# Opening of a fused two-layer transformer kernel: VectorE's work of the first token rounds reordered, setup work moved between rounds and engines, filler transposes on TensorE

## The reference, cut to what matters

```
x = x + xattn0(ctx, layernorm(x), mask, ...)   # heads 8 x 64; queries from x, keys and values from ctx and x; l2norm of q and k
x = x + int8_ffn(layernorm(x), weight_q, ...)  # per-row quantised 128x128 product
x = x + xattn1(layernorm(x), ctx, We, W2)      # softmax over the query axis
x = x + moe_ffn(layernorm(x), Wr, W1, W2, ...) # argmax over 8 experts, 128 -> 512 -> 128 with relu
```

```
def layer_norm(x, w, b): ... (x - mu) * rsqrt(var + LN_EPS) * w + b
def l2norm(t): t / max(sqrt(sum(t*t)), L2_EPS)
q = latents @ Wq ; k, v = split(concat([x, latents]) @ Wkv)
q = l2norm(q) * q_scale ; k = l2norm(k) * k_scale
out = softmax(where(mask, q k^T * SCALE, -max)) v ; layer_norm(out @ Wo)
```

## Time and profile before

| | |
|---|---|
| median of 3 runs | 961.88 us |
| the profiled execution | 963.69 us |
| its span in the trace | 962.0 us |
| TensorE busy | 913.5 us, 95% of the span |
| VectorE, ScalarE, GpSimd busy | 748.6, 691.3, 464.9 us |
| chain of waits, share on TensorE | 69% |

### The profile page before, as it was taken

How to read it: one execution, slowest core, us unless ns; L and a number is a source line. 1 busy time by engine, 2 the same in 40 slices (tenths; PEclk the granted TensorE clock), 3 DMA queues, 4 the chain that set the end, 5 groups by cost and what they waited for, 6 DMA issues and landing times.

```text
span 962.0 us, 30865 instructions
## 1 busy us (share of the span) xinstructions
PE 913.5 (95%) x11222; PEld 802.9 (83%) x11222; DVE 748.6 (78%) x2524; ACT 691.3 (72%) x1655; POOL 464.9 (48%) x1093
## 2 busy tenths in 40 slices
PE   3899999999999999999999999999999999899997
PEld 2688888888888888888888888888888878899997
DVE  4666788888888888888888888888888878868553
ACT  2777778777777777777777777777778766676764
POOL 4333333454545454544454444445453544767554
PEclk9999999999999999999999999999999999999999
DMA  6742000000000000000000000000000012246310
GB/s 180 219 132 38 2 3 1 3 13 3 13 2 13 3 10 5 14 2 8 7 11 5 8 7 8 7 8 8 8 8 7 8 47 70 60 90 111 96 52 21
DMA packets 45195, 31.45 MB, mean 33 GB/s; under 512 B 11556, under 2 KB 40167, under 8 KB 45047
## 3 DMA queue, kind: packets, MB, share of 16 engines
q1 hardware_dynamic: 39446, 19.93, 8.9%
q0 software_dynamic: 4320, 8.50, 2.8%
q10 hardware_dynamic: 1280, 1.05, 0.4%
HBM read 17.75 MB, written 12.17 MB: 31 GB/s over the span
## 4 chain that ended last, share of the span: by engine, by line
PE 69%; DVE 15%; ACT 9%; issue 3%; POOL 2%; SPq 1%; DMA 0%; DVEq 0%; POOLq 0%; ACTq 0%
PE ps L1622 9%; PE ps L1579 7%; PE ps L1554 7%; PE ps L1668 7%; PE ps L1533 5%; PE ps L1541 5%; PE ps L1376 5%; PE ps L1378 5%; PE ps L1377 5%; DVE sumsq L1271 4%; PE ps L1627 3%; ACT qk_hat L595 2%; PE ps L1652 2%; ACT probs L588 2%; PE ps L1415 1%
## 5 line engine op out<-in xcount | busy, mean ns | idle before, releaser
L1579 PE MATMUL ps<-v_x,prob 128*64 128x65 f32 x2048 | 130.6, 227 | 6.3 <-ACT qq_t L646 2.8
L655 ACT ACTIVATE prob<-ps,neg_shift 128x512 f32<-128x512 f32 x128 | 88.4, 691 | 67.0 <-PE ps L1622 66.8
L1271 DVE TENSOR_REDUCE sumsq<-qk_hat 128x8 f32<-128x512 f32 x168 | 108.4, 678 | 32.9 <-ACT qk_hat L595 30.6
L1303 DVE TENSOR_TENSOR qk_hat<-ps,rstd 128x512 f32<-128x512 f32 x168 | 106.3, 684 | 33.5 <-POOL rstd L826 32.6
L819 POOL TENSOR_TENSOR rs_t<-rs_y 128x32 f32<-128x32 f32 x73 | 17.7, 242 | 226.3 <-ACT rs_y L634 226.3
L1579 PEld LDWEIGHTS ps<-v_x,prob 128*64 128x64 f32 x2048 | 104.9, 137 | 25.2 <-issue 14.1
L1579 PE MATMUL ps<-v_c,prob 128*64 128x65 f32 x2048 | 125.7, 222 | 0.0
L1376 PE MATMUL ps<-w_hi,xc_hi 128*128 128x512 f32 x272 | 119.0, 438 | 2.4 <-POOL xc_lo L793 2.4
L595 ACT ACTIVATE qk_hat<-ps 128x512 f32<-128x512 f32 x168 | 98.7, 599 | 29.9 <-PE ps L1378 22.5
L1622 PE MATMUL ps<-qT_all,kT_all 64*128 64x128 f32 x1536 | 111.6, 285 | 2.9 <-ACT w_all L604 1.2
L1378 PE MATMUL ps<-w_hi,xc_lo 128*128 128x512 f32 x272 | 107.6, 395 | 0.0
(11 more groups left out here) (237 smaller groups left out, 2260.5 us busy)
## 6 DMA issues: line engine op xcount, KB each, us to landing
x_res<-sorted_rows SPq DMA_DIRECT2D x71, 65.5 KB
w_all<-in_L_ffn_W_dram SPq DMA_DIRECT2D x16, 256.0 KB, 4.8
sorted_rows<-fill SPq DMA_DIRECT2D x8, 327.5 KB
out_dram<-prob,x_res POOLq DMA_INDIRECT x71, 2.3
sorted_rows<-stage,idx POOLq DMA_INDIRECT x64, 2.4
ctx_res<-in_ctx_dram SPq DMA_DIRECT2D x8, 115.5 KB
x_res<-in_x_dram SPq DMA_DIRECT2D x1, 768.0 KB
sorted_rows<-fill SPq DMA_DIRECT2D x1, 524.0 KB, 5.1
```

What stands on the lines that cost most here:

```text
L655: nc.scalar.activation(prob[:, n // 2, n % 2 * INNER:(n % 2 + 1) * INNER], ps_s[n], ACT.Exp, bias=(mask_now[:, par:par + 1] if n > 1 else ...
L1271: nc.vector.reduce_sum(sumsq[:, n * H:(n + 1) * H], sq[:, n * INNER:(n + 1) * INNER].rearrange("p (h d) -> p h d", d=DH), AX).then_inc(ss_ ...
L1303: nc.vector.tensor_tensor(qk_hat[:, n * INNER:(n + 1) * INNER].rearrange("p (h d) -> p h d", d=DH), ps_qk[:, n, :].rearrange("p (h d) -> p ...
L1579: last = nc.tensor.matmul(dst[half:half + DH, :], prob[:, kt, col + half:col + half + DH], v, start=kt == 0, stop=kt == 1)
```

## The change

VectorE: `split_weights` is cut in two. The cast to `w_hi` waits until GpSimd has written the first variance (`var_ready` 1); `w_lo` is made after block 0's `xc_hat`, in three instructions of 512 columns. Statistics of block 2 and the sums of squares of block 0 move from round -1 to the end of round -2's middle part, ahead of the wait for `rs_ready` 2 and ahead of `xc_hat` of block 1. The copies of the turned expert weights are shared out anew: VectorE takes numbers 2 and 3, ScalarE 0, 1, 4 and 5, number 0 before the logarithm of round -1, 1 behind it, 4 and 5 at the end of the round.

TensorE: turns of experts 0 and 1 come before the transposes of `xc_hat` of block 1. The three transposes of the second layers, with ScalarE's copies of them, move from round 0 to round `SECOND_J` = 5. The wait for `setup_v` 12 moves to the second v product of round 0; ScalarE waits for `setup_v` 10 only. `keep_busy(48)` and `keep_busy(14)` issue transposes of the identity into PSUM bank 0 before round -2 and before round -1.

GpSimd: the memset of lot 2's context moves between the variance and the Newton step of round -1, the constants of the second layers behind that Newton step. SP: `arrived(1)` moves up from behind expert 2 to behind expert 1.

```diff
@@ SP
             for e in range(AHEAD):
                 expert(e)
-            arrived(1)
+                if e == 1:
+                    arrived(1)
@@ ScalarE
-            def first_weights():
+            def first_weights(some):
                 for n, bank, w in first_flips():
-                    if n > 1:
+                    if n in some:
                         act.wait_ge(s["wT_done"], n + 1)
                         nc.scalar.activation(w, ps[:, bank, :], ACT.Copy).then_inc(s["w_copied"], 1)
...
                 if not inside and j == 0:
-                    act.wait_ge(setup_v, SETUP_V)
+                    act.wait_ge(setup_v, SHIFT_V)          # 10
...
+                if not inside and j == -1:
+                    first_weights((0,))
                 roots()
...
                 if not inside and j == -1:
-                    first_weights()
+                    first_weights((1,))
...
+                if not inside and j == -1:
+                    first_weights((4, 5))
@@ GpSimd
                     last.then_inc(var_ready, 1)
+                    if not inside and j == -1:
+                        nc.gpsimd.memset(ctx_res[:, packed[2], :], 0.0).then_inc(ctx_zeroed, 1)
...
                     nc.gpsimd.tensor_tensor(rstd[:, par, :], rs_t4[:, :], rs_t3[:, :], ALU.mult).then_inc(rs_ready, 1)
+                if not inside and j == -1:
+                    second_setup()                         # L860 to L869 of before
                 if inside or j != -2:
                     high_low()
...
             run(-2, 0, 0, -2, False, -2, 0)
-            nc.gpsimd.memset(ctx_res[:, packed[2], :], 0.0).then_inc(ctx_zeroed, 1)
-            ...
@@ VectorE
-            def split_weights():
+            def high_weights():
                 dve.wait_ge(ld_qkv, 32)
+                dve.wait_ge(var_ready, 1)
                 nc.vector.tensor_copy(w_hi[:, :], w_raw[:, :]).then_inc(setup_v, 1)
+            def low_weights():
                 dve.wait_ge(setup_v, 2)
-                nc.vector.tensor_tensor(w_lo[:, :], w_raw[:, :], w_hi[:, :].bitcast(F32), ALU.subtract).then_inc(setup_v, 1)
+                for n in range(3):
+                    part = slice(n * INNER, (n + 1) * INNER)
+                    last = nc.vector.tensor_tensor(w_lo[:, part], w_raw[:, part], w_hi[:, part].bitcast(F32), ALU.subtract)
+                last.then_inc(setup_v, 1)
...
+            def sums_of_squares(j, pos):
+                for n in range(3) if fresh(pos + 1) else range(2):
+                    dve.wait_ge(sq_done, 3 * j + 4 + n)
+                    nc.vector.reduce_sum(...).then_inc(ss_raw, 1 if n == 0 or fresh(pos + 1) else 2)
+                dve.wait_ge(ss_raw, 3 * j + 6)
+                if j == -1:
+                    dve.wait_ge(rs_ready, 2)
+                nc.vector.tensor_scalar(var_in[:, 0:3 * H], sumsq[:, :], L2_EPS * L2_EPS, None, ALU.max).then_inc(ss_done, 1)
+            def third_tokens():
+                dve.wait_ge(tokens_in, 3)
+                nc.vector.bn_stats(bn6[:, 0, :], one(x_res, 2)).then_inc(xc_bn, 1)
+                dve.wait_ge(xc_bn, 3)
+                nc.vector.bn_aggr(xc_stat[:, 0, 0, :], bn6[:, 0, :]).then_inc(xc_mv, 1)
...
                 if not inside and j == -3:
-                    split_weights()
+                    high_weights()
                 if not inside and j == -2:
                     scales()
+                    third_tokens()
+                    sums_of_squares(-1, -1)
...
                     last.then_inc(hat_ready, 1)
+                if not inside and j == -3:
+                    low_weights()
@@ TensorE
-                if not inside and j == 0:
+                if not inside and j == SECOND_J:
                     pe.wait_ge(s["setup_d"], 1)
-                    pe.wait_ge(s["w_copied"], 4)
-                    pe.wait_ge(setup_v, SETUP_V)
                     nc.tensor.transpose(g_three[:, 0, :], wq_f, ident[:, :])
...
                     for kt in (0, 1) if fresh(pos) else (0,):
+                        if not inside and j == 0 and kt == 1:
+                            pe.wait_ge(setup_v, SETUP_V)
...
+                if not inside and j == -1:
+                    first_weights((0, 1, 2, 3))
                 if has(j + 2, inside):
                     pe.wait_ge(hat_ready, j + 3)
...
+            def keep_busy(n):
+                for i in range(n):
+                    nc.tensor.transpose(ps[:, 0, 0:P], ident[:, :], ident[:, :])
+
             pe.wait_ge(setup_g, FIRST_G)
             run(-3, 1, 3, -3, False, -3, 0)
+            keep_busy(48)
             run(-2, 0, 0, -2, False, -2, 0)
+            keep_busy(14)
...
-                    for n, bank, w in first_flips():
-                        pe.wait_ge(ld_exp[n // 2], 32)
-                        if n > 3:
-                            pe.wait_ge(s["w_taken"], n - 3)
-                        flip(bank, w).then_inc(s["wT_done"], 1)
-                    pe.wait_ge(s["w_copied"], 1)
+                    first_weights((4, 5))                  # waits w_copied 1, 2
+                    pe.wait_ge(s["w_taken"], 1)
                     pe.wait_ge(setup_v, 4)
```

More of the change, by code:

```diff
@@ L304, in whole @@
         SETUP_V, SETUP_G, FIRST_G = 12, 9, 7
+        SHIFT_V = 10
+        SECOND_J = E - AHEAD
         SETUP_P = 10
@@ L730, in _, with second_setup @@
             pool.wait_ge(setup_g, FIRST_G)
+            def second_setup():
+                nc.gpsimd.memset(upper_f, 1.0).then_inc(setup_p, 1)
+                nc.gpsimd.iota(rev_i[:, :], pattern=[[-1, E]], base=E, channel_multiplier=0).then_inc(setup_p, 1)
+                nc.gpsimd.iota(part_i[:, :], pattern=[[PART, E]], base=0, channel_multiplier=0).then_inc(setup_p, 1)
+                nc.gpsimd.iota(table["iota_i"][:, :], pattern=[[1, table["iota_i"].shape[1]]], base=0,
+                               channel_multiplier=0).then_inc(setup_p, 1)
+                nc.gpsimd.iota(table["base_i"][:, :], pattern=[[PART, E]], base=0, channel_multiplier=0).then_inc(setup_p, 1)
+                nc.gpsimd.memset(before[:, :], 0.0).then_inc(setup_p, 1)
+                nc.gpsimd.memset(ones_pp[:, :], 1.0).then_inc(setup_p, 1)
+                pool.wait_ge(setup_p, 7)
+                nc.gpsimd.affine_select(out=upper_f, in_=upper_f, compare_op=ALU.is_gt, fill=0.0,
+                                        base=0, pattern=[[1, P]], channel_multiplier=-1).then_inc(setup_p, 1)
             def store(k):
@@ L1220, in run @@
                     dve.wait_ge(o_bn, j - 1)
-                if has(j + 3, inside):
+                if has(j + 3, inside) and (inside or j != -1):
                     dve.wait_ge(tokens_in, j + 4)
@@ L1237, in run @@
                                                    lno_w[:, :], ALU.subtract, ALU.mult).then_inc(o_cent, 1)
-                elif has(j + 3, inside):
+                elif has(j + 3, inside) and (inside or j != -1):
                     dve.wait_ge(xc_bn, j + 4)
-                if has(j + 3, inside):
+                if has(j + 3, inside) and (inside or j != -1):
                     for n in (0, 1) if fresh(pos + 3) else (0,):
@@ L1267, in run @@
                     first_table(j, 0)
[L1268 to L1272, removed]
-                                             AX).then_inc(ss_raw, 1 if n == 0 or fresh(pos + 1) else 2)
-                    dve.wait_ge(ss_raw, 3 * j + 6)
-                    nc.vector.tensor_scalar(var_in[:, 0:3 * H], sumsq[:, :], L2_EPS * L2_EPS, None,
-                                            ALU.max).then_inc(ss_done, 1)
+                if has(j + 1, inside) and (inside or j != -1):
+                    sums_of_squares(j, pos)
                 if not tail(j, inside):
@@ L1390, in flip, with first_weights @@
                 return last
+            def first_weights(some):
+                for n, bank, w in first_flips():
+                    if n in some:
+                        pe.wait_ge(ld_exp[n // 2], 32)
+                        if n > 3:
+                            pe.wait_ge(s["w_copied"], n - 3)
+                        flip(bank, w).then_inc(s["wT_done"], 1)
             def slot_a(j, rho, g, inside):
-                if not inside and j == 0:
+                if not inside and j == SECOND_J:
                     pe.wait_ge(s["setup_d"], 1)
-                    pe.wait_ge(s["w_copied"], 4)
-                    pe.wait_ge(setup_v, SETUP_V)
                     nc.tensor.transpose(g_three[:, 0, :], wq_f, ident[:, :])
@@ L1503, in three_emptied @@
                     pe.wait_ge(s["w_copied"], 4 + 2 * j + 2)
+                if not inside and j == SECOND_J:
+                    pe.wait_ge(s["setup_c"], 3)
                 for at, name, of in ((0, "place_done", g - 2), (1, "pr_done", g - 1), (2, "qt_copied", g),
```

9 lines of the change are left out of this document (7 added, 2 removed).

## The result

The changed kernel takes 959.0 us (median of 6 runs, 957.82 to 959.71) against 963.13 us of the kernel before (6 runs beside it on the same chip): ratio 0.9961, 95% interval 0.995 to 0.9971, so 2.8 to 4.8 us faster. The forecast of 956.9 us was counted from a median of three runs, 961.88; beside the changed kernel, with six runs, the kernel before has 963.13, so 1.25 us of the distance between 956.9 and 959.0 lie in the starting point and 0.9 in the gain. On two other chips the gain was 4.0 us (977.97 against 981.92, ratio 0.9957, 0.9941 to 0.9973) and 3.5 us (980.25 against 983.71, ratio 0.9956, 0.9942 to 0.9969). The profiled execution takes 959.33 us, its span is 957.6 us, 4.4 less than before.

What follows compares the result with a forecast made beforehand. Opening bound by a chain of latencies up to the first v product at 28.28 us, TensorE afterwards; 5.9 - 0.5 - 0.4 = 5.0 us gained, 961.88 - 5.0 = 956.9 us; range 955.4 to 961.0, the forecast's own 956.0 to 958.5.

Steps and rivals of the forecast that it cites:

- part 5: Round 0 on TensorE: a stall of 0 to 1.1 us for expert 3's second load, taken as -0.4 us.
- Part 1: Weight split leaves GpSimd's first variance undisturbed: first Newton step 2.0 us earlier, block 0's products 2.1 us earlier.
- Part 2: Fillers raise TensorE's clock early: block 0's nine passes take 2.1 instead of 3.7 us, `var_in` 4.1 us earlier.
- rival 1: The filler transposes never raise TensorE's clock: gain only 1.0 us, 960.9 us; chance 0.15.
- rival 2: TensorE's clock rises, then falls in the gaps before block 0's products: gain 3.8, 958.1 us; chance 0.11.
- Rivals 3 and 4: Fillers each wait for the last's drain, 963.0 us, chance 0.06; GpSimd's disturbance only moved, 958.0 us, 0.09.
- Parts 3 and 4: VectorE fills the Newton wait, `qk_hat` 4.1 us earlier; setup leaves round 0, v product 5.9 us earlier, round 5 loses 0.5.
- The slip of SP: Moving `arrived(1)` ahead of expert 2 delays everything behind it on SP by 0 to 1.0 us, taken as 0.5.
- the landing: Expert 3's second load takes 4.8 us from issue to landing, so it lands at 23.3 to 23.8 us.

Runs made afterwards that it cites:

- the undisturbed trace: The changed kernel itself run again on another chip, its clock not dropping in the opening: 977.97 us, against 981.92 for the kernel before.

## Why the prediction was right, and where it was off

It said 5.0 us; the medians give 4.1, 4.0 and 3.5, and a pair of traces without clock stretches in the opening 3.6. The mechanism was right: the v product came early, by the links named, and a short wait for expert 3 took part of it back. The term that was mis-sized most is that wait, part 5. By its steps:

- Part 1, 2.0 us at the Newton step: 1.6. The variance was written at 7.8 as worked out, and GpSimd was not slowed by VectorE (0.1 us of the gain is that lot 0 came earlier in this trace). The term was mis-sized because I took ScalarE as free at 7.9, and its queue held mask loads until 8.40. Before, the late variance had hidden them.
- Part 2: the products came at 14.2 (forecast 13.9), at the high level, `var_in` at 17.91 (17.73). The clock rose under transposes alone, so rival 1 fell; the Trainium skill (TensorE: Matmul & The Clock Gate, "Part 4: PE-mode transpose") has it that they don't count as work, and here the measurement decides against it. (The trace lists these transposes as MATMUL and does not show their mode.) When the rise comes differs from trace to trace: the 48 fillers took 6.95 to 8.25 us in the ten traces that have them, 8.19 in the profiled one. By 0.22 and 0.11 us each, and 0.16 us of drain, that is an estimate of 3.0 to 5.6 us of fillers at the low level; the forecast had 3.1, the early end. Its 1.4 us of margin was 0.5 to 1.8. The shortest and the longest:

```profile
2.54 6.95 PE L1727 MATMUL ps<-ident 128*128 128x128 f32 x48 [2.54 <-POOL lift_bias L735]
2.55 8.25 PE L1725 MATMUL ps<-ident 128*128 128x128 f32 x48 [2.55 <-POOL lift_bias L735]
```

- The one idle microsecond before the products did not bring the clock down, so rival 2 did not happen in the changed kernel. But it did happen with the split undone, behind 2.83 us of idle time (above). So part 1, which shortens that idle time, may also be what keeps the clock up for part 2.
- Rivals 3 and 4 did not happen either: fillers that write one address start 0.11 us apart at the high level, and the cast (7.91 to 8.87) was over before the Newton step; of the token split only the cast, beside the last piece of `w_lo`, took longer, 0.49 instead of 0.40 us.
- Parts 3 and 4: `qk_hat` at 20.24 (19.9); first v product 5.44 us earlier (5.9, counted from the chain's 28.28 where the row has 28.04). Round 5 lost 0.5 us, as said: in the undisturbed trace the lead over the kernel before goes from 3.67 us at `rstd` of round 4 to 3.19 at round 9. Between there and the first expert tile it grows again to 3.6; where that comes from was not looked into.
- Part 5 is the step that failed in size: a stall of 1.5 to 1.8 us instead of 0.4, beyond my bound of 1.1. The slip of SP, taken as 0.5, was -0.06, 0.05 and 0.58 us in the three traces of the changed kernel (expert 3's second load was issued at 18.43, 18.54 and 19.07, before at 18.49). The term that was wrong is the landing: I used the median of sixteen loads, 4.8 us, and this load took 7.3, 7.1 and 6.8 us. That could have been read before the run: in the trace of the kernel before, the same load alone, from its issue at 18.49, shows

```profile
DMA to landing us min/median/max: 6.6/6.6/6.6
```

So it landed near 25.1, and against the 23.8 at which I had TensorE come this gives a stall of 1.3 us before any slip. In every trace where it is issued at this place it took 6.1 to 7.3 us. Lot 2's 768 KB and its context were being issued right behind it in all of them. That these slow it is not shown: the early load was moved away from them and ahead of other loads at once.
- The drop of the clock near 32 us, 1.3 to 1.4 us in four of the twelve traces of kernels with the new order, was in none of my terms (a fifth, with the split undone, dropped at 13 us instead). I had tied it to the wait for expert 3 when I set up the experiments; that theory fell: the drop came in two traces without the wait, and stayed away in one with a wait of 1.50 us. What decides it stays open: TensorE rows that were the same for 7.7 us went either way. One trace of the kernel before and one of it with fillers are too few to say that the old order never had it.

The parts were worked out one behind the other and added, and the sum came out 0.9 to 1.5 us too high; it stayed in its range because the wait at the end of the chain was one of its terms, if too small. But with expert 3 landing at 25.7 us, parts 1, 2 and 4 had only the time up to there to gain together. Undone one at a time they cost 0 (part 1), 0.1 to 0.4 (fillers) and -0.5 us (part 4); the 5.4 us that they bring together at the v product are 3.75 at `rstd` of round 0, behind that one load.

## What to carry to other kernels

When a chain of latencies is shortened, list every load that the stretch behind it needs, with its own landing time, read for this one load in the trace (6.6 us here), not the median of its kind (4.8): the chain can't be shortened past it, and one reordered issue (1.6 to 1.8 us here) was worth more than any of the three edits undone alone. Undoing one part tells only what that part is worth while the others stand. Before a difference between two traces is explained, line up a mark that both have, round by round: here half of it arose 800 us from the change. And check the clock in every stretch of every run: a drop at 13 us changed what one of the experiments here seemed to cost.

## What the runs showed of the hardware

- The granted clock fell to the low level near 32 us in four of the twelve traces of kernels with the changed order, for 3 to 4 us, at a cost of 1.3 to 1.4 us, among them one of two whose TensorE rows were the same to 0.02 us for the 7.7 us before. In a fifth it fell at 13 us, after 2.83 us without work.
- Transposes of an fp32 identity alone raised the clock, in ten traces of ten. The rise came after some 3.0 to 5.6 us of them (estimated from 6.95 to 8.25 us for 48). Products vary too: it came after 3.1 us of them in the kernel before, and in the two traces without fillers shown above nine products in a row, 0.43 us apart and 4.0 us together, all ran at the low level.
- GpSimd's instruction of 0.19 us took 0.74 beside VectorE's cast in SBUF and 1.71 us beside its two-input subtraction, in the kernel before and in the changed kernel with the split undone.
- The same program (the changed kernel) needed 154.6 us from its first expert tile to the end on one chip and 176.5 us on another, with that tile at 803.03 and 803.02 us. The second trace has there three stretches of 3 to 7 us at the low clock, of which the first has none before its last microseconds, and 33 us of waits, summed over ScalarE and VectorE, that the profile puts down to "remote", of which the first has none. What those are stays open.
